# One projection for queries, keys and values over five PSUM banks, with attention one slot later and the key sum behind it

## The reference

```python
x = x + _conv_bn(x, dw0_w, dw0_s, dw0_b, groups=C)            # 3x3 depthwise
x = x + _ffn(x, f0_w1, f0_s1, f0_b1, f0_w2, f0_s2, f0_b2)     # 64 -> 128 -> 64, relu
x = x + _windowed_attn(x, wq, wkv, pos, scale_p, dwc_w, dwc_b, proj_w, proj_b)
x = x + _conv_bn(x, dw1_w, dw1_s, dw1_b, groups=C)
x = x + _ffn(x, f1_w1, f1_s1, f1_b1, f1_w2, f1_s2, f1_b2)

# attention of one window: N = 49 tokens, C = 64
q = xw @ wq.T;  k = xw @ wkv[:C].T + pos;  v = xw @ wkv[C:].T
q = (relu(q) + 1e-06) / sc;  k = (relu(k) + 1e-06) / sc
q, k = _focus(q), _focus(k)         # t**3 scaled back to the norm of t
z = 1 / (q . k.sum(tokens) + 1e-06)             # per head
y = (q @ (k.T @ v)) * z + depthwise5x5(v) + dwc_b
out = y @ proj_w.T + proj_b
```

## Time and profile before

| | |
|---|---|
| time, median of 3 runs | 200.72 us (199.43 to 200.98) |
| time of the profiled execution | 198.42 us |
| its span in the trace | 196.7 us |
| PE busy | 182.4 us (93%), 1938 matmul records |
| DVE busy | 129.3 us (66%) |
| ACT busy | 96.4 us (49%) |
| POOL busy | 36.8 us (19%) |
| granted PE clock | 1.00 in every slice |
| chain that ended last | PE 75%, DVE 10%, ACT 4%, DMA 4%, issue 4% |

### The profile page before, as it was taken

The page is one execution under the profiler, slowest core; times in us unless marked ns, Lnnn a source line. Parts: engine busy times, 40 slices in busy tenths (PEclk is TensorE's granted clock), DMA queues, the critical chain, the costliest instruction groups (busy, mean ns, idle before and its releaser), DMA issues.

```text
span 196.7 us, 4705 instructions
## 1 busy us (share of the span) xinstructions
PE 182.4 (93%) x1938; PEld 99.4 (51%) x1938; DVE 129.3 (66%) x235; ACT 96.4 (49%) x152; POOL 36.8 (19%) x78
## 2 busy tenths in 40 slices
PE   7989996999999999999999999999999997999882
PEld 6424441447547546973574475376458553532220
DVE  3746895796899998066997889699694464041111
ACT  2473544493394296429518815842856124333430
POOL 1000053018009009000720450180081000000000
PEclk9999999999999999999999999999999999999999
DMA  6999945942000000000530261171064018766912
GB/s 144 223 261 209 206 81 125 220 103 57 0 2 3 3 0 0 3 3 0 154 73 7 69 154 57 57 170 53 3 165 111 3 59 224 172 160 155 283 35 80
DMA packets 15092, 19.12 MB, mean 97 GB/s; under 512 B 2160, under 2 KB 10608, under 8 KB 15072
## 3 DMA queue, kind: packets, MB, share of 16 engines
q1 hardware_dynamic: 13744, 17.63, 37.7%
q10 hardware_dynamic: 1328, 1.20, 2.6%
HBM read 14.50 MB, written 4.33 MB: 96 GB/s over the span
## 4 chain that ended last, share of the span: by engine, by line
PE 75%; DVE 10%; ACT 4%; DMA 4%; issue 4%; SPq 0%; POOL 0%; DVEq 0%; POOLq 0%
PE ps L471 19%; PE ps L606 9%; PE ps L495 9%; PE ps L558 6%; PE ps L512 4%; PE ps L660 4%; PE ps L489 4%; PE ps L666 3%; PE ps L623 3%; PE ps L577 3%; PE ps L562 3%; DMA xr<-x_out 3%; PE ps L516 2%; DVE x L863 2%; DMA x_out<-x 2%
## 5 line engine op out<-in xcount | busy, mean ns | idle before, releaser
L471 PE MATMUL ps<-xr,dwst 96*32 96x480 f32 (+1 forms) x384 | 42.8, 579 | 0.8 <-DMA xr<-x_out 0.5
L320 POOL TENSOR_SCALAR vmt<-vbot,cst 128x128 f32<-128x128 f32 x48 | 19.6, 428 | 110.7 <-ACT vbot L352 110.7
L344 ACT ACTIVATE hid<-ps,fst 128x512 f32<-128x512 f32 x32 | 20.3, 687 | 13.7 <-PE ps L489 13.7
L471 PEld LDWEIGHTS ps<-xr,dwst 96*32 96x32 f32 x384 | 11.0, 109 | 28.4 <-issue 27.0
L382 ACT ACTIVATE kv<-ps,cst 128x288 f32<-128x288 f32 x32 | 19.8, 790 | 6.2 <-PE ps L562 6.2
L495 PE MATMUL ps<-hid,w2t 128*64 128x512 f32 x64 | 21.1, 616 | 1.5 <-ACT hid L344 1.5
L359 ACT ACTIVATE sq<-tqk 128x1280 f32<-128x1280 f32 x8 | 10.2, 1270 | 24.1 <-DVE tqk L779 23.4
L489 PE MATMUL ps<-x,w1t 64*128 64x512 f32 x64 | 18.1, 640 | 2.6 <-ACT x L336 1.7
L751 DVE SCALAR_TENSOR_TENSOR y<-ps,fst,x 128x512 f32<-128x512 f32 x8 | 6.0, 750 | 21.2 <-PE ps L495 21.1
L606 PEld LDWEIGHTS ps<-qt,kv 64*64 64x64 f32 x576 | 17.4, 135 | 4.9 <-issue 4.8
L336 ACT ACTIVATE x<-ps,fst 128x512 f32<-128x512 f32 x16 | 11.0, 685 | 17.4 <-PE ps L471 16.9
(11 more groups left out here) (105 smaller groups left out, 248.1 us busy)
## 6 DMA issues: line engine op xcount, KB each, us to landing
xr<-x_out SPq DMA_DIRECT2D x16, 264.0 KB, 4.6
xr<-in_x SPq DMA_DIRECT2D x16, 240.0 KB, 6.0
x_out<-x SPq DMA_DIRECT2D x8, 272.0 KB, 2.1
xr<-x_out SPq DMA_DIRECT2D x8, 272.0 KB, 3.4
xr<-in_x SPq DMA_DIRECT2D x8, 256.0 KB, 5.0
out<-y SPq DMA_DIRECT2D x8, 256.0 KB, 2.2
tband<-in_matrix ACTq DMA_DIRECT2D x1, 784.0 KB, 6.8
wts<-in_weights SPq DMA_DIRECT2D x1, 416.0 KB, 7.5
```

The source lines that it names most:

```text
L320: last = eng.tensor_scalar(vmt[:, w, :, :], vbot[:, g, :, :], cc("win_bot")[:, w:w + 1], 0.0, ALU.mult, ALU.add)
L344: eng.activation(hid[:, m % 2, a, :], bank(P_H + a), ACT.Relu, bias=ff(f"f{s}b1")).then_inc(h_ready, 1)
L471: last = eng.matmul(dst[:, :, max(-dx, 0):HW - max(dx, 0)], dwst[:, s, tile % 2, dx + 1, :], taps_of(m, tile, dx), start=(dx == 0), stop=( ...
```

## The change

Queries, keys and values of a group come out of one projection. The block-diagonal weight tile grows from 4 to 6 blocks of 64 columns (DVE copies `wv` into it at the start), and ten matmuls (eight of 192 columns, two of 384) write banks 3 to 7, two slots in a bank. They take the place of 22 matmuls. `take_v` reads its values there, after DVE has read queries and keys, and moves to the head of ACT's slot. Since banks 6 and 7 now hold values until `take_v` has read them, `key_sum` waits for `take_v` of the next group (`v_ready`). `attend` moves one slot back, writes bank 0 instead of bank 7, and stands between the projection and `key_sum`; `take_y` moves with it. `ffn2(n+2)` leaves the end of slot n and becomes `ffn2(n+1)` behind `key_sum`, `residual` likewise on DVE; conv(m) waits for `residual(m-1)`. `turn_q` and `ffn1` end the slot; `window_conv` stands ahead of them and waits for `attended(3)` in slot 8. On ACT `hidden` and then `ratio` end the slot. `project` is renamed `project_out`.

```diff
-        P_DW, P_H, P_QK, P_V = 0, 1, 3, 6
+        P_DW, P_H, P_QKV, P_KS = 0, 1, 3, 6
...
-        DW_BANK = [0, 7] + [0] * 10 + [5, 6, 7, 0]
+        DW_BANK = [0, 3] + [0] * 10 + [5, 6, 7, 0]
...
+        def ffn_bank(m):
+
+            return bank(DW_BANK[m] if m > 1 else 0)
+
+        def qkv():
+
+            return ps[:, 512 * P_QKV:512 * (P_QKV + 5)].rearrange("p (s n) -> p s n", s=NS)
...
             def take_v(g):
-                eng.wait_ge(v_ps, g + 1)
-                src = ps[:, 512 * P_V:512 * P_V + 1024].rearrange("p (a n) -> p a n", a=2)
+                eng.wait_ge(kraw_ready, g + 1)
+                eng.wait_ge(tq_ready, g + 1)
+                src = qkv()[:, :, 2 * C:3 * C]
                 eng.activation(vband[:, g, :, :].rearrange("p (t a) c -> p a t c", a=2),
...
             eng.wait_ge(c_in, 16)
             for n in range(2, LAST):
                 g1, g2 = n - 1, n - 2
+                if n > 2:
+                    take_v(g1)
+                    take_y(g2 - 1)
                 squares(g1)
+                sixth(g1)
                 take_kv(g2)
                 widened(n + AHEAD)
-                sixth(g1)
-                take_v(g1)
-                hidden(n + AHEAD)
-                take_qt(g2)
-                ratio(g1)
                 for k in FM_SLOTS.get(n, []):
                     take_fm(k)
-                take_y(g2)
+                take_qt(g2)
+                hidden(n + AHEAD)
+                ratio(g1)
+            take_y(NG - 2)
+            take_kv(NG - 1)
             widened(LAST + AHEAD)
-            take_kv(NG - 1)
             take_qt(NG - 1)
...
-                elif m == 2:
-                    eng.wait_ge(res_ready, 1)
-                elif 2 < m < 12:
+                elif 2 <= m < 12:
                     eng.wait_ge(res_ready, m)
...
-                if n > min(FM_SLOTS):
-                    eng.wait_ge(fm_ready, chunks_before(n))
+                if m == 2:
+                    eng.wait_ge(pads_taken, 1)
+                if n >= min(FM_SLOTS):
+                    eng.wait_ge(fm_ready, chunks_before(n + 1))
                 if FM_FIRST <= n < LAST:
                     eng.wait_ge(x3_ready, n - FM_FIRST + 1)
...
-                    last = eng.matmul(dw_bank(m)[64 * a:64 * a + 64], w2t[:, s, :], hid[:, m % 2, a, :], start=True, stop=True)
+                    if m == 1 and a == 0:
+                        eng.wait_ge(res_ready, 1)
+                    if 4 <= m < 12 and a == 0:
+                        eng.wait_ge(y_ready, m - 3)
+                    last = eng.matmul(ffn_bank(m)[64 * a:64 * a + 64], w2t[:, s, :], hid[:, m % 2, a, :], start=True, stop=True)
                 last.then_inc(f_ps, 1)
...
-            def project_qk(g):
+            def project_qkv(g):
                 if g == 0:
                     eng.wait_ge(qk_ready, 1)
+                    eng.wait_ge(x1_ready, 2)
...
+                    eng.wait_ge(v_ready, 2)
                 if g >= 2:
                     eng.wait_ge(kv_ready, g - 1)
+                    eng.wait_ge(prod_ready, g - 1)
+                    eng.wait_ge(qt_ready, g - 1)
                 for t in range(4):
                     at = PX * (t % 2) + TOK * (t // 2)
                     for a in range(2):
                         p = slice(64 * a, 64 * a + 64)
-                        o = 512 * (P_QK + a) + TC * t
-                        eng.matmul(ps[:, o:o + TC], x2[p, g, at:at + 128], wqk[p, 2 * a:2 * a + 2, :],
-                                   start=True, stop=True)
-                for j in range(GP):
-                    at, o = PX * j + PX - 64, 512 * (P_QK + 2)
-                    last = eng.matmul(ps[64 * j:64 * j + 64, o:o + 2 * TC], x2[:, g, at:at + 64],
-                                      wqk[:, :, :].rearrange("p s c -> p (s c)"), start=True, stop=True)
-                last.then_inc(qk_ps, 1)
...
-            def project_v(g):
-                if g == 0:
-                    eng.wait_ge(res_ready, 2)
-                if g >= 1:
-                    eng.wait_ge(prod_ready, g)
-                for t in range(4):
-                    at = PX * (t % 2) + TOK * (t // 2)
-                    for a in range(2):
-                        p = slice(64 * a, 64 * a + 64)
-                        o = 512 * (P_V + a) + C * t
-                        eng.matmul(ps[:, o:o + C], x2[p, g, at:at + 128], ww("wv")[p], start=True, stop=True)
+                        eng.matmul(qkv()[:, 4 * a + t, 0:3 * C], x2[p, g, at:at + 128],
+                                   wqk[p, 3 * a:3 * a + 3, :].rearrange("p s c -> p (s c)"), start=True, stop=True)
                 for j in range(GP):
                     at = PX * j + PX - 64
-                    for a in range(2):
-                        p = slice(64 * a, 64 * a + 64)
-                        o = 512 * (P_V + a) + 4 * C
-                        last = eng.matmul(ps[64 * j:64 * j + 64, o:o + C], x2[p, g, at:at + 64], ww("wv")[p],
-                                          start=True, stop=True)
-                last.then_inc(v_ps, 1)
+                    last = eng.matmul(qkv()[64 * j:64 * j + 64, 8:10, 0:3 * C], x2[:, g, at:at + 64],
+                                      wqk[:, :, :].rearrange("p s c -> p (s c)"), start=True, stop=True)
+                last.then_inc(qkv_ps, 1)
...
             def key_sum(g):
                 eng.wait_ge(kf_ready, g + 1)
-                eng.wait_ge(v_ready, 2 * (g + 1))
-                if g == 0:
-                    eng.wait_ge(projc_read, 1)
-                    eng.wait_ge(pads_taken, 1)
-                if g >= 1:
-                    eng.wait_ge(qt_ready, g)
-                    eng.wait_ge(y_ready, g)
-                o = 512 * P_V
+                eng.wait_ge(v_ready, 2 * min(g + 2, NG))
...
             def attend(g):
                 eng.wait_ge(kv_ready, g + 1)
                 eng.wait_ge(qt_ready, g + 1)
+                eng.wait_ge(x1_ready, g + 2 * AHEAD + 1)
...
-                                dst = ps[p, 512 * (P_V + 1) + PX * j:512 * (P_V + 1) + PX * j + PX]
+                                dst = ps[p, PX * j:PX * j + PX]
...
+                eng.wait_ge(h_ready, 2 * (4 * half + 4 + AHEAD))
+                if half == 1:
+                    eng.wait_ge(x3_ready, 4)
...
             conv(2)
-            project_qk(1)
             ffn1(2)
-            project_v(0)
+            project_qkv(1)
             ffn2(2)
-            pad_sums()
             conv(3)
             ffn1(3)
-            ffn2(3)
             for n in range(2, LAST):
                 g1, g2, c = n - 1, n - 2, n - FM_FIRST
                 if n > 2:
-                    project_qk(g1)
+                    project_qkv(g1)
+                    attend(g2 - 1)
+                key_sum(g2)
+                ffn2(n + AHEAD - 1)
                 if 0 <= c:
                     turn_fm(c)
-                key_sum(g2)
                 key_value(g2)
                 conv(n + AHEAD)
                 if 0 <= c:
-                    project(c)
-                project_v(g1)
-                ffn1(n + AHEAD)
-                turn_q(g2)
-                ffn2(n + AHEAD)
+                    project_out(c)
                 for k in FM_SLOTS.get(n, []):
                     window_conv(k)
-                attend(g2)
+                turn_q(g2)
+                ffn1(n + AHEAD)
+            attend(6)
+            key_sum(7)
+            ffn2(10)
             turn_fm(4)
-            key_sum(7)
-            project(4)
+            key_value(7)
+            project_out(4)
             conv(11)
             turn_fm(5)
-            key_value(7)
-            project(5)
+            turn_q(7)
+            project_out(5)
             turn_fm(6)
-            turn_q(7)
-            project(6)
+            project_out(6)
             ffn1(11)
...
             k_raw(0)
             q_t(0)
+            residual(1)
             k_t(0)
...
+            eng.tensor_copy(kf[96:128, 0:8, :], bank(P_H)[96:128, 448:512].unsqueeze(1).broadcast_to([32, 8, C]))
+            eng.tensor_copy(kf[0:32, 8:10, :], bank(P_H)[0:32, 448:512].unsqueeze(1).broadcast_to([32, 2, C])).then_inc(pads_taken, 1)
             cubes(0)
             norm2(0)
+            residual(2)
             k_raw(1)
             q_t(1)
             k_t(1)
-            residual(2)
             norm6(0)
...
             k_focus(0)
-            residual(3)
...
                     k_raw(g1)
                     q_t(g1)
                     k_t(g1)
-                if 0 <= c:
-                    add_fm(c)
                 if n == 3:
                     spread_taps(1).then_inc(taps_ready, 1)
                     scale_ffn(1)
                 q_dot(g2)
+                cubes(g1)
                 q_sum(g2)
-                cubes(g1)
+                residual(n + AHEAD - 1)
                 if 0 <= c:
-                    attended(c)
+                    add_fm(c)
                 q_scale(g2)
                 q_final(g2)
                 norm2(g1)
```

(6 more changed lines are left out.)

70 lines of the change are left out of this document (34 added, 36 removed).

## The result

The changed kernel takes 208.47 us (median of four runs, 206.52 to 209.26) where the kernel before, beside it on the same chip, takes 200.37 (199.43 to 200.98). The ratio is 1.047, with a 95% interval of 1.041 to 1.054: slower, as forecast, but by 8 to 9 us and not by 5. The median lies at the upper edge of the range given (208.5); by the ratio, 200.7 x 1.047 = 210.2, it lies above it. The profiled executions are 198.42 us before (span 196.7) and 207.92 after (span 206.0), 9.3 us of span apart.

What follows compares the result with a forecast made beforehand. PE's own list was taken to set the pace before the change; after it, a chain through all engines. Start 0.3, slots 0.2, tail 1.7 and 2.9 sum to +5.1: 200.7 + 5.1 = 205.8 us, range 201.8 to 208.5.

Steps and rivals of the forecast that it cites:

- The new wait of 1.6 us before `q_dot`: In each slot, DVE idles 1.6 us before `q_dot` because `key_sum` now waits for `take_v`.
- The projection at 2.10: On PE, the merged projection takes 2.10 us, bounded by 1.7 and 3.1; up to 2.9 costs a late slot nothing.
- ACT's order, `ratio` behind `hidden`: At the slot's end, `ratio` starts at `hidden`'s end, not when DVE's norms are ready, and `k_focus` waits for it.
- Late slots 16.34: Walked from one `k_raw` to the next, a late slot takes 16.34 us, against 16.24 before.
- The term of the masks: GpSimd's masks keep costing 0.15 us in each slot, now on `q_scale` and `q_final` instead of `k_focus`.
- the sum: Whole kernel: start 0.3, slots 0.2, tail 1.7 and 2.9 make +5.1 us, some 2.5%.
- Rival 3: GpSimd's masks hold up `q_scale` and `q_final` in four late slots, adding 3.6 us: 209.4, in full 213.0; chance 0.13.
- the walk: The changed kernel's slot followed link by link from `k_raw`: early slot 15.23 us, slot 4 20.00, late slot 16.34.
- The start, +0.3: Up to the third slot, which starts 0.3 us later; bounded by -0.5 and +1.5.
- The tail, +1.7 and +2.9: Last `k_raw` to `key_sum(7)` grows by 1.7 us, and `key_sum(7)` to `ffn1(11)` by 2.9 us.
- The matmuls saved pay for the new wait, no more: Slots 3 to 7 together change by only +0.2 us.

Runs made afterwards that it cites:

- experiment 6: The changed kernel with its projection cut in two again at the same place, queries and keys first, then values: 210.2 us, ratio 1.043.
- experiment 3: The changed kernel with `ratio` ahead of `hidden` on ScalarE, nothing else: 201.89 us, ratio 1.010.
- experiment 1: The changed kernel with two idle matmuls of 256 columns in PE's wait before each key sum from the third slot on: 205.22 us, ratio 1.024.
- experiment 9: The changed kernel with `ratio` before `hidden`, the tail in the old order and `widened(3)` before `ratio(0)`: 200.55 us, ratio 1.004.
- experiment 10: The kernel of experiment 9 with two idle matmuls of 256 columns in PE's wait before each key sum from the third on: 200.43 us.
- experiment 8: The changed kernel with only its last stretch written in the old order: 206.68 us, ratio 1.029.
- experiment 12: The changed kernel with `ratio` before `hidden`, values copied first, old tail, `widened(3)` before `ratio(0)`, and the last key sum ahead of `attend(6)`: 198.90 us, ratio 0.9988.

## Why the prediction was right and wrong

- **The new wait of 1.6 us before `q_dot`**: 1.63. Right, and with it every link up to the conv, within 0.08 us.
- **The projection at 2.10**: 2.22 (from 101.29 to the start of `attend` at 103.51). Right, and PE's busy time in a late slot fell by the forecast 1.0 us (15.77 to 14.71). That its length does not matter in a slot is nearly right: 0.8 us more of it cost 0.2 (experiment 6).
- **ACT's order, `ratio` behind `hidden`**: right; experiment 3 takes it away and gets 0.4 to 0.5 us per slot.
- **Late slots 16.34**: 16.54 at clock 1.00. The term of the masks was mis-sized: I carried 0.15 us over, and it was 0.38 to 0.40 on `q_scale` and `q_final`, with `k_focus` giving back 0.13 for which the sum had nothing. Rival 3's mechanism exists, but it asked for 0.9 us per late slot (3.6 in four) and got 0.4, of which 0.2 is net.
- **The step that failed** is the walk's tacit assumption that PE's waits are free because PE is not the bound. "PE has finished projection and `attend` by then" was true and was the fault: PE stood idle for 1 us ahead of the key sum, the granted clock then fell to 0.50 in slots 4, 5 and 7 (and in slot 2 behind the wait for `widened(3)`), and for 3.4 us (6.8 in slot 2) the matmuls on the chain took up to twice as long. That is 1.1 us in slots 5 and 7 each, 0.9 in slot 4 (20.79 against 19.87), about 0.5 in the start: 3.6 of the 4.2 us by which the sum was short. Experiment 1 gives 3.2 us back; that the clock held in its slot 2 as well is not the fillers' doing.
- **The start, +0.3**: +0.95, of which about 0.5 is the clock (50.18 in experiment 1). The other 0.4 is near the walk. The ratio of group 0 ahead of `widened(3)` is a dear part of it: experiment 9 moves it and gains 0.94, with a fall of the clock in slot 2, and experiment 10, where the clock held there, starts its third slot at 48.32.
- **The tail, +1.7 and +2.9**: +1.83 and +2.73. The size was right. That its written order was to blame, which I came to believe after the result, fell with experiments 8 and 12: the old order gives 0.6 us at most, an early key sum 0.8. From the last `k_raw` to `ffn1(11)` all the orders together win 2.1 of the 4.6 us back (37.17 to 35.06, before 32.61). For the 2.5 that stay, the attention of one more group, left to do when the last projection is through, is a reading of the program text; no run isolates it.
- **"The matmuls saved pay for the new wait, no more"**: in the slots the change can win, 0.3 us each, once ACT and the copy are put in another order. As written the late slots are 0.3 us longer than before even at clock 1.00 (16.54 against 16.24).

## What to carry to other kernels

When a change makes an engine wait that is not the bound, price the wait all the same: here TensorE's clock fell at a wait of about 1 us in 10 cases of 26, and the low clock then lay on the chain. The walk along the chain gave slots to about 0.2 us where the clock held, but it should list each matmul's clock as a term, with the row it is taken from. The stage moved one slot back cost 4.6 us once, at the drain, and the orders tried won 2.1 of it back.

## What the runs showed that I had not expected

- Two idle matmuls of 1.13 us in TensorE's wait made the kernel 3.2 us faster (208.47 to 205.22), and the same two ahead of the conv made each late slot 0.6 us longer (17.14 against 16.54, both at clock 1.00).
- The clock fell to 0.50 inside slots in which PE was busy for 92% of the time (16.25 of 17.68 us), behind a single wait of 0.99 us.
- A GpSimd copy of 0.69 us stretched one VectorE instruction on 40 columns from 0.18 to 0.62 us in slots 6 and 8, and in the slots where it started later it did not; six short ones in the same place stretched the same stretch of VectorE's work by 0.38 us in all.
